# The first two steps of an expert loop in another order, with its first row loads on two issuers

## The reference, cut to what matters

```
router_logits = x @ gate_w.T
scores = sigmoid(router_logits)
_, topk_ids = top_k(scores + e_bias, 4)
topk_w = scores at topk_ids, divided by their sum
g = einsum('th,ehi->tei', x, w1)        # 32 experts, 128 -> 96
u = einsum('th,ehi->tei', x, w3)
a = silu(g) * u * combine[:, :, None]
out = einsum('tei,eih->th', a, w2)      # 96 -> 128
x = x + gb * out
```

## Time and profile before

| | us |
|---|---|
| median of 3 runs | 689.37 |
| lowest, highest | 688.49, 689.84 |
| the profiled execution's own time | 688.63 |
| its span, first to last instruction | 686.7 |

### The profile page before, as it was taken

One profiled execution on the slowest core, in us unless ns is written; L12 is line 12 of the kernel. 1 busy time (PEld: TensorE's weight loads), 2 busy tenths in 40 slices (PEclk: granted clock), 3 DMA queues, 4 the chain that ended last, 5 costly groups with the idle time before them and its releaser, 6 DMA issues.

```text
span 686.7 us, 16134 instructions
## 1 busy us (share of the span) xinstructions
PE 481.4 (70%) x4426; PEld 371.9 (54%) x4427; DVE 454.3 (66%) x1486; ACT 315.2 (46%) x683; POOL 389.8 (57%) x606
## 2 busy tenths in 40 slices
PE   2568888888888776677766764222999999981057
PEld 0235555555555554565545553211899889980046
DVE  5776888888887774477786778850466666662028
ACT  0346777777787763432333323301566556430000
POOL 5565666666665400047676767773277777777700
PEclk9968999999999999977877876555999999995569
DMA  7996000000006006001111111145354545421178
GB/s 204 297 261 165 3 0 0 0 0 0 0 1 247 2 1 184 1 30 57 53 55 51 53 53 56 62 134 150 102 149 128 148 128 148 127 85 50 53 305 314
DMA packets 68850, 66.26 MB, mean 96 GB/s; under 512 B 8912, under 2 KB 60336, under 8 KB 68800
## 3 DMA queue, kind: packets, MB, share of 16 engines
q1 hardware_dynamic: 52096, 43.64, 21.5%
q0 software_dynamic: 8192, 17.84, 7.4%
q10 hardware_dynamic: 8512, 4.20, 2.1%
HBM read 40.86 MB, written 27.93 MB: 100 GB/s over the span
## 4 chain that ended last, share of the span: by engine, by line
DVE 26%; PE 25%; issue 22%; POOL 10%; DVEq 6%; ACT 6%; DMA 3%; POOLq 1%; SPq 1%; ACTq 0%
DVE L L1289 6%; PE PS L1046 5%; POOL xs L637 4%; POOL ys L655 3%; PE PS L931 3%; DVE yidx L1678 3%; PE PS L1137 2%; PE PS L1058 2%; PE PS L1206 2%; PE PS L906 2%; DVEq L335 2%; DVE YQ L1676 1%; PE PS L954 1%; POOL QKR L535 1%; PE PS L1069 1%
## 5 line engine op out<-in xcount | busy, mean ns | idle before, releaser
L637 POOL DMA_INDIRECT xs<-YQ,posi x128 | 124.9, 976 | 109.3 <-issue 98.3
L655 POOL DMA_INDIRECT ys<-YQ,yidx x128 | 122.6, 958 | 60.6 <-issue 34.2
L1289 DVE TENSOR_TENSOR L<-PS,BIAS 128x768 f32<-128x768 f32 x128 | 116.6, 952 | 39.0 <-PE PS L934 33.3
L703 ACT ACTIVATE PR<-L 128x768 f32<-128x768 f32 x128 | 106.0, 842 | 60.7 <-DVE L L1289 58.6
L1676 DVE SCALAR_TENSOR_TENSOR YQ<-PS,tag,YQ 128x128 f32 x160 | 56.2, 351 | 46.1 <-DVE yidx L1678 29.7
L1137 PE MATMUL PS<-BIAS,V 128*128 x320 | 64.1, 346 | 3.7 <-issue 1.6
L931 PE MATMUL PS<-YQ 32*128 32x256 f32 x512 | 47.3, 439 | 27.2 <-DVE L L1289 25.7
L1137 PEld LDWEIGHTS PS<-BIAS,V 128*128 128x128 f32 x320 | 53.0, 196 | 10.8 <-issue 10.8
L1046 PE MATMUL PS<-YT,w1s 128*128 128x256 f32 x128 | 42.3, 487 | 15.8 <-ACT YT L767 15.8
L1058 PE MATMUL PS<-w2s,hid 128*128 128x128 f32 x256 | 36.3, 300 | 14.5 <-ACT hid L771 14.5
L931 PEld LDWEIGHTS PS<-YQ 32*128 32x128 f32 x512 | 20.9, 188 | 46.8 <-DVE L L1289 33.1
(11 more groups left out here) (256 smaller groups left out, 1114.2 us busy)
## 6 DMA issues: line engine op xcount, KB each, us to landing
PR<-xs SPq DMA_DIRECT2D x160, 72.0 KB
BIAS<-ys SPq DMA_DIRECT2D x12, 512.0 KB, 8.2
modb<-mod_rows SPq DMA_DIRECT2D x1, 4096.0 KB, 14.0
dist_rep<-dist_row SPq DMA_DIRECT2D x4, 768.0 KB, 7.8
xs<-pad_row SPq DMA_DIRECT2D x33, 72.0 KB, 12.4
xs<-pad_row SPq DMA_DIRECT2D x1, 2304.0 KB, 17.8
X<-in_x ACTq DMA_DIRECT2D x4, 512.0 KB, 6.6
BIAS<-dist_rep SPq DMA_DIRECT2D x4, 512.0 KB, 8.6
```

The source lines that it names most:

```text
L637: pool.indirect_dma_start(out=xs, out_offset=bass.IndirectOffsetOnAxis(ap=posi[j][:, t * TOPK + k:t * TOPK + k + 1], axis=0), in_=ROWS[j][ ...
L655: pool.indirect_dma_start(out=ys, out_offset=bass.IndirectOffsetOnAxis(ap=yidx[:, n:n + 1], axis=0), in_=YQ[:, n * D:(n + 1) * D], in_offs ...
L703: act.activation(PR[u % 4][:, :], L[u % 2][:, :], ACT.Exp).then_inc(s["exp_done"], 1)
L1289: return dve.tensor_tensor(L[u % 2][:, :].rearrange("p (j w) -> p j w", j=2), PS[:, at:at + 2, 0:HW], BIAS[:, u, :].rearrange("p (j w) -> ...
```

## The change

It has four parts.

- **Order.** The first two steps are written in the order of their data on PE, ACT and DVE, and the loop's order begins with step 2. On PE `down(0)` and `down(1)` stand before `rows_T(2)` and `rows_T(3)`.
- **Row loads.** Of the first eight row DMAs, SP issues those of tiles 0 and 1 of each buffer, ACT those of tiles 2 and 3. ACT loads eight row numbers into registers and waits for the same semaphores as SP.
- **Silu table.** ACT runs a silu on one element before it waits for the row numbers.
- **Waits of POOL.** The table `passes_of` has one entry for each of the 128 tiles rather than for each group of four. Tiles 0 to 3 of each life are waited for one by one; from tile 4 on POOL waits before each group of four for its last tile, as before. The table's constants need one iota on POOL instead of two.

```diff
-            for j, first in enumerate((YGROUP - 1, YGROUP + 2 * XG)):
-                pool.iota(group_no[:, j:j + 1], [[0, 1]], base=first, channel_multiplier=YGROUP, ...)
+            pool.iota(passes_no[:, :], [[0, 1]], base=1 + 2 * XG, channel_multiplier=1, ...)
...
-            def load_pair(rows, buf):
-                for j in range(2 * XG):
+            def load_pair(rows, buf, half=range(2 * XG)):
+                for j in half:
...
-            load_pair(first, 0)
+            load_pair(first, 0, [j for j in range(2 * XG) if j % XG < XG // 2])
             load_pair(second, 2)
...
             def y_rows(life):
+                def after_passes_of(n):
+                    passes = pool.value_load(passes_of[:, bass.ds(life * SLOTS + n, 1)], ...)
+                    pool.wait_ge(s["y_ev"], passes)
+                    settle(pool)
+                for n in range(SLOTS):
+                    if n < YGROUP:
+                        after_passes_of(n)
+                    elif n % YGROUP == 0:
+                        after_passes_of(n + YGROUP - 1)
+                    pool.indirect_dma_start(out=ys, ...)
...
             clear(0)
             clear(1)
+            act.activation(sg[0][0:1, 0:1], zero[0:1, :], ACT.Silu)
+            act.wait_ge(s["t_ready"], 1)
+            rows = load_many(mybir.EngineType.Activation, treg[0:1, 2:4, :]..., 0, DUMMY)
+            for i in range(GROUP):
+                act.wait_ge(s[f"scat{i}"], 16 * NT * TOPK // GROUP)
+            act.wait_ge(s["pad_done"], 16 * NE)
+            for j in range(2 * XG):
+                if j % XG >= XG // 2:
+                    act.dma_start(xg[j // XG][:, j % XG, :], xs[bass.ds(rows[j], P), :]).then_inc(...)
             rows_ev(0, 0)
+            silu(0, 0)
             rows_ev(1, 1)
-            silu(0, 0)
-            for i in range(XSTEPS):
+            a_T(0, 0)
+            silu(1, 1)
+            rows_ev(2, 0)
+            a_T(1, 1)
+            clear(2)
+            silu(2, 0)
+            rows_ev(3, 1)
+            clear(3)
+            for i in range(2, XSTEPS):
                 step(i)
...
                 if first:
-                    behind = []
+                    begin = experts(0, 1)
+                    rows_T(0, 0, 0)
+                    gate_up(0, 0, begin)
+                    rows_T(1, 1, 0)
+                    a_T(0, 0)
+                    gate_up(1, 1, ahead)
+                    down(0, 0, begin)
+                    rows_T(2, 2, 0)
+                    a_T(1, 1)
+                    now = experts(2, 1)
+                    gate_up(2, 0, now)
+                    down(1, 1, ahead)
+                    rows_T(3, 3, 0)
+                    ahead = experts(3, 1)
...
-                for n in range(8):
+                for n in range(2 if first else 0, 8):
                     ... gate_up(m + 1), rows_T(m + 2), a_T(m) as before ...
-                    if not first or n > 0:
+                    if not first or n > 2:
                         down(m - 1, 1 - par, behind)
...
-            st(dve.tensor_scalar(gt[:, :], edge[:, 0, :], group_no[:, 0:1], None, ALU.is_le))
+            st(dve.tensor_scalar(gt[:, :], edge[:, 0, :], tile_no[:, 0:1], None, ALU.is_le))
...
-            for i in range(2):
-                rows_ev(i, i, first=True)
+            rows_ev(0, 0, first=True)
             act_mul(0, 0)
-            for i in range(4):
+            rows_ev(1, 1, first=True)
+            act_mul(1, 1)
+            y_evac(0, 0, 0)
+            rows_ev(2, 2, first=True)
+            act_mul(2, 0)
+            y_evac(1, 1, 1)
+            rows_ev(3, 3, first=True)
+            for i in range(2, 4):
                 step(i, i)
```

More of the change, by code:

```diff
@@ L197, in build @@
         place_no = sb("place_no", [P, NT * TOPK])
-        group_no = sb("group_no", [P, 2])
+        passes_no = sb("passes_no", [P, 1])
         cnt = sb("cnt", [P, NE])
@@ L486, in _ @@
                       allow_small_or_imprecise_dtypes=True)
-            for j, first in enumerate((YGROUP - 1, YGROUP + 2 * XG)):
-                pool.iota(group_no[:, j:j + 1], [[0, 1]], base=first, channel_multiplier=YGROUP,
-                          allow_small_or_imprecise_dtypes=True)
+            pool.iota(passes_no[:, :], [[0, 1]], base=1 + 2 * XG, channel_multiplier=1, allow_small_or_imprecise_dtypes=True)
             pool.memset(zero[:, :], 0.0)
@@ L645, in y_rows @@
             def y_rows(life):
[L646 to L657, removed]
+                def after_passes_of(n):
+                    passes = pool.value_load(passes_of[:, bass.ds(life * SLOTS + n, 1)], min_val=1, max_val=XG * (XSTEPS + 2))
+                    pool.wait_ge(s["y_ev"], passes)
[5 more added lines that the diff above has]
+                        after_passes_of(n + YGROUP - 1)
+                    pool.indirect_dma_start(
+                        out=ys, out_offset=bass.IndirectOffsetOnAxis(ap=yidx[:, n:n + 1], axis=0),
+                        in_=YQ[:, n * D:(n + 1) * D], in_offset=None).then_inc(s[f"yst{n // 16}"], 16)
             pool.wait_ge(s["tw_ready"], 1)
@@ L857, in _ @@
             clear(1)
+            act.activation(sg[0][0:1, 0:1], zero[0:1, :], ACT.Silu)
+            act.wait_ge(s["t_ready"], 1)
+            rows = load_many(mybir.EngineType.Activation, treg[0:1, 2:4, :].rearrange("p a b -> p (a b)"), 0, DUMMY)
+            for i in range(GROUP):
[3 more added lines that the diff above has]
+                if j % XG >= XG // 2:
+                    act.dma_start(xg[j // XG][:, j % XG, :], xs[bass.ds(rows[j], P), :]).then_inc(s[f"x_rows{j // XG}"], 16)
             rows_ev(0, 0)
+            silu(0, 0)
             rows_ev(1, 1)
-            silu(0, 0)
-            for i in range(XSTEPS):
+            a_T(0, 0)
[7 more added lines that the diff above has]
+            for i in range(2, XSTEPS):
                 step(i)
@@ L1163, in experts, with eight_steps @@
                 return load_many(mybir.EngineType.PE, e_of, i * XG, NE - 1, n * XG)
-            def eight_steps(i, turn, now=None, ahead=None, left=XSTEPS):
-                first = now is not None
+            def eight_steps(i, turn, first=False, left=XSTEPS):
+                ahead = experts(i + 1, 1)
                 if first:
-                    behind = []
+                    begin = experts(0, 1)
[12 more added lines that the diff above has]
+                    ahead = experts(3, 1)
                 else:
-                    ahead = experts(i + 1, 1)
                     behind = experts(i - 1, 1)
                     now = experts(i, 1)
-                for n in range(8):
+                for n in range(2 if first else 0, 8):
                     m, par = i + n, n % 2
@@ L1185, in eight_steps @@
                         ahead = experts(m + 2, 1)
[L1186 to L1190, removed]
+            eight_steps(0, 0, first=True)
             with pe.Fori(1, XSTEPS // 8 - 1) as eight:
@@ L1641, in _ @@
             st(dve.tensor_scalar(wsum[:, :], wsum[:, :], float(YROWS // P), None, ALU.min))
-            st(dve.tensor_tensor(tv[:, 6:7], rk[:, 2:3], group_no[:, 1:2], ALU.add))
+            st(dve.tensor_tensor(tv[:, 6:7], rk[:, 2:3], passes_no[:, :], ALU.add))
             st.wait()
@@ L1685, in step @@
                     rows_ev(i + 2, (n + 2) % 4, first=at(i, 0, 1))
-                if not at(i, 0):
+                if not at(i, 2):
                     y_evac(i - 1, (n + 1) % 2, (n + 3) % 4)
-            for i in range(2):
-                rows_ev(i, i, first=True)
+            rows_ev(0, 0, first=True)
             act_mul(0, 0)
-            for i in range(4):
+            rows_ev(1, 1, first=True)
[6 more added lines that the diff above has]
+            for i in range(2, 4):
                 step(i, i)
```

## The result

| | before | after |
|---|---|---|
| median, us (8 runs each) | 689.52 | 691.60 |
| lowest to highest | 688.49 to 690.51 | 690.42 to 692.62 |
| ratio, 95% interval | | 1.0025 (1.0014 to 1.0036) |
| profiled execution / its span | 688.63 / 686.7 | 690.42 / 688.4 |

The change makes the kernel 2.1 us slower, with an interval of 1.0 to 2.5. The forecast was +1.0, a time of 690.4 us; 691.60 lies within the whole range (688.4 to 692.0) and 0.2 above the range that the prediction gave to its own forecast (689.6 to 691.4).

What follows compares the result with a forecast made beforehand. The end was taken as pass 10 plus a constant, POOL's scatters following without a gap. Start -0.80, gaps +1.20 and clock +0.55 gave about +1.0 on the median 689.37: 690.4 us, own range 689.6 to 691.4, whole range 688.4 to 692.0.

Steps and rivals of the forecast that it cites:

- POOL sets the end, pass 10 sets POOL: DVE's pass 10 (an expert's part added to a slot) releases tile 4's `ys` scatter; then POOL runs gapless, 1.263 us each.
- Tile by tile waits worth nothing: POOL's `ys` scatters: the first comes earlier, but tile 4 still waits for pass 10; extra waits lie under running scatters: 0.
- Silu table worth nothing: ACT's 1.28 us table load, hidden under PE's gate/up product, moves to idle time at 446: 0.
- Loads 0.80: First row loads split over SP and ACT: PE starts 0.80 us earlier, taken between 0.70 and 1.05.
- The lower price, 0.70: Gain of the split row loads if two issuers take 0.70 us a pair: 4 x 0.524 - 4 x 0.35.
- The order: PE's first steps up to down 2, listed one by one: new gaps 3.20 us in sum, +1.20 against the old order.
- The clock's rise left at 482.84: PE's clock rises when it did before; with PE starting earlier, 6.8 us instead of 6.0 run at low clock: +0.55.
- The sum: Start -0.80, gaps +1.20, clock +0.55: pass 10 and tile 4's scatter +0.95 to +1.0 us later.
- The gaps did not close: Rival, chance 0.18: PE's gaps of 0.88 to 0.94 each lose 0.2 to 0.3, or the clock rises earlier; 688.6 to 689.4.
- the second issuer did bring something: Its opposite was a rival, chance 0.16: buffer 0 lands as before, PE pays all new gaps, +1.5 us, 690.9.
- PE did not fall back to its low clock: The fall was a rival, chance 0.07: two nearby gaps of 0.9 drop PE's clock, 1.5 to 2 more, about 692.
- That POOL's start is the bound: Rival, chance 0.07: tile 4 needs no pass 10, all scatters move with the first, 6.0 and 0.41 earlier: 683.0 us.

Runs made afterwards that it cites:

- `after_waits16`: The changed kernel with tiles 0 to 15 of each life waited for one by one, in place of 0 to 3; 688.44 us, ratio 0.9980 to before.
- `silu_again`: The kernel before with only the silu on one element ahead of the loop, in the group where before took 811.3 us; ratio 1.0015.

## Why the prediction came out as it did

- **POOL sets the end, pass 10 sets POOL.** Right: 0.79 from pass 10 to tile 4 in all three undisturbed profiles with the coarse wait, 1.263 between scatters, and `after_waits16` moved the end by the 3.8 worked out.
- **Tile by tile waits worth nothing.** Right by the traces (times don't settle it), with one flaw: two such waits in a row are not wholly hidden. Ahead of tile 2's and 3's scatters stand 0.52 and 0.37 us, not 0.30, 0.29 more in sum; ahead of tile 2's it is 0.53 to 0.57 in the three other undisturbed runs with single waits. It fell into the wait before tile 4; in the kernels with 16 waits the later ones show 0.30.
- **Silu table worth nothing.** Right (`silu_again`, by its trace).
- **Loads 0.80.** Mis-sized: 0.61 (475.91 - 472.08 = 3.83 from the landing of the last `xs` scatter to PE's start before, 476.19 - 472.97 = 3.22 after). The lower price, 0.70, rested on issues that stretch to 0.70 us when SP and ACT issue together; here they began together, at 473.27 and 473.29, and SP's took 0.33 to 0.40, ACT's 0.36 to 0.40. So the issue came 1.05 earlier, the upper bound. What the sum left out is the landing, which took 0.4 to 0.5 longer with two queues. In other undisturbed runs PE's start was 0.35 to 0.46 earlier than before (5.64 to 5.75 against 6.10).
- **The order.** Right in place: gaps of 0.88, 0.06, 0.44, 0.88 and 0.94 were forecast, 0.93, 0.32, 0.45, 0.92 and 0.92 came. From PE's start to pass 10 the list of steps had 496.51 + 1.43 - 475.10 = 22.84, and 22.84 came. That it came out so exactly is luck, since terms were off and cancelled: the first gate/up took 2.72 at the low clock until the next transposes began (480.96 - 478.24), not 2.50, and the gap before a(0) was 0.26 longer; but then more of gate/up 1 ran behind the clock's rise (it took 1.50, not 1.91). Work that slips past the rise runs at the high clock, so a delay ahead of it costs less than its length.
- **The clock's rise left at 482.84.** Right in this pair: 13.0 us after the last `xs` scatter began, before and after, though PE started 0.61 earlier on that scale. Luck has a part in it, since in two of the other four undisturbed profiles it came at 11.7 and 11.6.
- **The sum.** +0.95 to +1.0 was forecast for tile 4's scatter, +1.28 measured. The sum had lost about 0.1 against its own list of steps, which gives 496.51 - 495.43 = +1.08, and the loads' missing 0.19 makes up the rest. The median's +2.1 is more than either. Its interval reaches down to +1.0, and the profiled pair has 0.9 from the kernel's unchanged start; whether the rest is chance or something the profiles don't show stays open. So the case fell on the slower side of 0.2%, to which I gave 0.29, and above what I called the forecast's own range.
- **The rivals.** The gaps did not close, the second issuer did bring something, and PE did not fall back to its low clock (the granted clock was 1.00 in each stretch of 2 us from 484 to 500). That POOL's start is the bound was wrong for this kernel. It is right with the old order and fine waits, where POOL runs through from its first scatter; in the new order with fine waits 3.54 us before tile 7 are left.

## What to carry to other kernels

When an engine runs without a gap to the end, find the one event from which it does so, and judge each edit by what it does to that event; an earlier first piece is worth nothing if the second waits for the same thing as before. A pipeline's staggered order costs latency in the first steps but covers the hand-overs (all but one of 0.92 us here); written in the order of the data, each hand-over through another engine (0.6 us of copy and 0.3 on the way here) stands open unless a product of another step lies in it. Where the consumer is the bound, wait for what a piece needs and not for the last of its group: twelve finer waits in each life moved the last scatter of the changed kernel by 3.8 us in the traces. And when two traces of one stretch are compared, look where the clock rose in each before a difference of half a microsecond is put down to the edit.

## What the runs showed of the hardware

- Two queues of the same core: eight loads of 72 KB from SP and ACT went out twice as fast, and the fourth of a buffer landed 2.31 to 2.52 us after its issue, not 1.84 to 1.90. Of 1.05 us won at the issue 0.35 to 0.61 arrived at PE's start.
- PE's clock went from 1.2 to 2.4 GHz between 5.7 and 7.5 us after PE's first work of the loop (5.66, 5.80, 6.93, 7.31, 7.36 and 7.52 in six profiles). Counted from the start of the last `xs` scatter it was 13.0 in four of them and 11.7 and 11.6 in two, and PE's earlier start with split loads did not bring it forward. Between two profiles of one order the rise alone moved pass 10 by 0.44.
- A gate/up product by itself holds PE 2.72 us at the low clock; of two back to back each takes about 2.5 (an estimate, 3.77 us for 1.51 of them).
- In two of three groups of runs the same kernel took 811 to 818 us instead of 690, with stops that the profile puts down to no instruction of the core (the longest 9.5 us in the first group, 14.4 in the third), while POOL's busy time stayed at 389.0 to 390.7 us (389.8 before). Two of the groups, one of either kind, have the same chip number. Differences of one us can't be timed there.
